# Weighing with high and low halves, four places for u, and scalings at the end of a batch, in a fused cross-attention and expert kernel

## The chip, the cores and the metric

One core of a Trainium2 chip. The metric is device microseconds from launch to end; lower is better. Engines: PE multiplies (with a weight-load side, PEld), DVE is the vector engine, ACT the activation engine, POOL the GpSimd engine, and SP issues every DMA of this kernel.

## The reference

`x` is 32 batches of 128 tokens of width 128, `ctx` 32 batches of 128 context rows of width 64.

```python
x = x + tanh(g_xattn) * (softmax(heads(ln(x) @ Wq) @ heads(ctx @ Wk).T / 8) @ heads(ctx @ Wv) @ Wo + bo)   # 16 heads of 64
x = x + tanh(g_ffn) * (shared_mlp(ln(x)) + routed_mlp(ln(x)))   # 32 experts of width 64; 8 picked out of 2 of 4 groups
```

## The kernel before, in words

**The products are folded.** Wq and Wk are folded per head at the start, and so are Wv and Wo (`c_pair`). So for each batch the scores are `ctx` times a projection `g` of the normalised tokens; the weights `p = exp(scores - max)` are applied to the raw context rows (`ctx_keys`, with a column of ones that gives the sum of the weights); the result `u` is divided by its sum and multiplied with `c_pair`.

**Formats.** Most products are made of three fp32r products, high*high + low*high + high*low, of operands that were split beforehand (`split_product`, L1148). Two products take plain f32 operands: `weigh` (L1219, u = keys x p) and `project_out` (L1245). A plain f32 product appears in the trace as two matmul records.

**Stages.** After a set-up of some 20 us come eight chunks of CB = 4 batches (`attention`, written once for each engine). The first and the last chunk are written out; chunks 1 to 6 (24 batches) are the body of a hardware loop (`in_chunks`, L238), the steady chunks. Then eight chunks of 17 expert units follow (`experts_of`), from about 355 us on. Batches b = 1 and 3 of a chunk are called odd here, b = 0 and 2 even.

**The order of the work is written out by hand**; each engine runs its list in order, with semaphore waits. In batch t:

- PE (L1287): `max_scores` of t+2 for the first half of the heads (h = 0), `scores` of t for h = 0, `transpose_max` of t+1, `weigh` of t-1 for h = 1 (two products, q = 0 and 1), in b = 1 `transpose_norm`, `project_out` of t-3, `max_scores` and `scores` for h = 1, `weigh` of t for h = 0, q = 0; in odd batches `g_project` of the next chunk into banks 0 to 3; `weigh` of h = 0, q = 1. `g_project` waits for `take_max` and `exp`, which empty its banks. The products of the next batch that write into banks 0 to 3 wait until `g_low` has read them (`glo_ready`, L1181 and L1203).
- ACT (L605): two `exp_of` of h = 0, `max_out`, two `u_out` of t-1 for h = 1 (copies of u from its bank into `u_raw`), in b = 1 `xt_high`, two `exp_of` of h = 1, `u_out` of t for h = 0, q = 0, in odd batches four `g_high`, `u_out` of h = 0, q = 1. `u_raw` has two places, so `u_out` waits until `normalise` has read what was there two batches ago (L548).
- DVE (L997): two `take_max` (L788) for h = 0, `normalise` of t-2 for q = 0 (L802, u times the inverse sums), in b = 1 `xt_low`, two `take_max` for h = 1, `invert` of t-1 (L796), `normalise` of t-2 for q = 1, in odd batches four `g_low` (L780), `residual` of t-3, statistics; in b = 0 `ln_apply` of the next chunk.
- POOL (L497): splits the expert weights (L468) and the context (L457), adds a bias.
- SP (L350): `load_max_row` of t+1, `spread_sums` of t-1 (L297), loads of context, expert weights and keys, `store_inverse` and `spread_inverse` of t-1 (L310): the sums go through a small DMA to `sums`, DVE inverts them, they are stored to DRAM and read back spread over partitions into `inverse_bc`, which has one place. All these pass through one queue in order.

`wbc` (L169) holds routing weights in the expert stage and is idle in the attention stage; so are the second parts of `x2t_hi`, `x2t_lo`, and the last columns of `w_hi`, `w_lo` until the last chunk.

Of the kernel before, what the change touches and what calls it, by code (L numbers as in the profile page):

```python
# [28 lines left out]
ALU = mybir.AluOpType  # L29
AX_X = mybir.AxisListType.X  # L30

P = 128
# [37 lines left out]
STATS_AT = {2: (2,), 3: (3,), 4: (4,), 5: (5,), 6: (6, 7)}  # L70
NB_SEAM = (NCH - 2) * CB
SEAM = {4: (1, 6), 5: (6, 10), 6: (10, 14), 7: (14, 21)}
LATE = {NB - 2: 3, NB - 1: 12}
NORM_AT = {(9, 1): ((NB - 1, 0),), (10, 1): ((NB - 1, 1),)}


def build(nc, x, ctx_nat, ctx_t, g_xattn, g_ffn, wq_t, wk_t, wv_t, wo, bo, router_t, router_bias, experts, out):
    with ExitStack() as stack:
# [42 lines left out]
        u_raw = (u_even, u_odd)  # L121
# [33 lines left out]

        spare = sb("spare", [P, 2 * CB * NE])
# [12 lines left out]
        wbc = sb("wbc", [P, WBC_SLOTS, 2, CT])  # L169
        rows_dram = nc.dram_tensor("rows_dram", (NCH, NE, CT), F32, kind="Internal").ap()  # L170
# [32 lines left out]
        st_done, exp_ready = sem("st_done"), sem("exp_ready")  # L203
        u_done, u_ready, inverse_ready = sem("u_done"), sem("u_ready"), sem("inverse_ready")
        norm_ready = [sem("norm_even_ready"), sem("norm_odd_ready")]
        sums_in, inverse_out, inverse_in = sem("sums_in"), sem("inverse_out"), sem("inverse_in")
# [66 lines left out]
        def _(sp):  # L273
# [23 lines left out]
            def spread_sums(t, parity):  # L297

                wait_first(u_ready, 4 * t + 4)
                for q in range(2):  # L300
                    row = CD if q == 0 else 0
                    sp.dma_start(sums[rows(q), parity, :], u_raw[parity][row:row + 1, q, :, :]).then_inc(sums_in, 16)
# [7 lines left out]
            def spread_inverse(t, parity):  # L310

                wait_first(inverse_out, 16 * t + 16)
                for q in range(2):
                    wait_first(norm_ready[q], t)
                for q in range(2):
                    sp.dma_start(inverse_bc[rows(q), :, :].rearrange("p h n -> p (h n)"),
                                 inverse_dram[parity, q:q + 1, :].broadcast_to([HD, 2 * CT])).then_inc(inverse_in, 16)
# [32 lines left out]
            def attention(c, first, last):  # L350
                for b in range(CB):
# [3 lines left out]
                    if not (first and b == 0):  # L355
                        spread_sums(t - 1, (b - 1) % 2)
# [64 lines left out]
            spread_sums(NB - 1, (NB - 1) % 2)  # L421
# [21 lines left out]
        def _(pool):  # L443
# [23 lines left out]

            def split_weights(slot, t, nth, contexts):  # L468
# [28 lines left out]
            def attention(c, first, last):  # L497
                for b in range(CB):
                    t = CB * c + b
                    split_weights(b % 2, t, 2 * c + b // 2, NB if last else t + CB)  # L500
# [24 lines left out]
        def _(act):  # L525
# [19 lines left out]
            def u_out(t, parity, h, q):  # L545
# [4 lines left out]
                nc.scalar.activation(u_raw[parity][held, q, h, :], u_ps[q][held, :], ACT.Copy).then_inc(u_ready, 1)  # L550
# [53 lines left out]

            def attention(c, first, last):  # L605
                for b in range(CB):
# [11 lines left out]
                    if not last and b == 1:  # L618
                        xt_high(c + 1)
# [7 lines left out]
                    u_out(t, b % 2, 0, 0)  # L627
                    if b % 2 == 1 and not last:
                        g_high(2 * c + 2 + b // 2, b // 2)
                    u_out(t, b % 2, 0, 1)  # L630
# [11 lines left out]
            u_out(NB - 1, (NB - 1) % 2, 1, 0)  # L642
            nc.scalar.activation(gates[:], tanh_g[:], ACT.Silu)
            u_out(NB - 1, (NB - 1) % 2, 1, 1)
# [44 lines left out]
        def _(dve):  # L689
# [105 lines left out]

            def invert(t, parity):  # L796
# [5 lines left out]
            def normalise(t, parity, q):  # L802

                dve.wait_ge(inverse_in, 32 * t + 32)
                wait(dve, attn_done, t - 1)
                nc.vector.tensor_tensor(u_t[rows(q), parity, :, :].rearrange("p i n -> p (i n)"),  # L806
                                        u_raw[parity][rows(q), q, :, :].rearrange("p h n -> p (h n)"),
# [189 lines left out]
            def attention(c, first, last):  # L997
                for b in range(CB):
                    t = CB * c + b
                    for h in range(2):  # L1000
# [7 lines left out]
                        if h == 1:  # L1008
                            if first and b >= 2:
                                normalise(t - 2, b % 2, 0)  # L1010
                            if not (first and b == 0):
                                invert(t - 1, (b - 1) % 2)
                            if not (first and b < 2):
                                normalise(t - 2, b % 2, 1)
# [5 lines left out]
                        if h == 1 and b % 2 == 1 and not last:  # L1020
# [11 lines left out]
                        elif not last and step_of_chunk == 1:  # L1032
                            ln_apply(c + 1, t - b + CB)
# [9 lines left out]
                        if h == 0 and not first:  # L1043
                            normalise(t - 2, b % 2, 0)
                        if step_of_chunk == 2 and not last:
                            xt_low(c + 1)
# [6 lines left out]
            in_chunks(dve, attention)  # L1053
            residual(NB - 3)
            normalise(NB - 2, (NB - 2) % 2, 0)
            invert(NB - 1, (NB - 1) % 2)
            normalise(NB - 2, (NB - 2) % 2, 1)


            def levels_at(c, parity, u, place, first, last):  # L1060

                if first:
                    for t, q in NORM_AT.get((u, place), ()):
                        normalise(t, t % 2, q)
# [82 lines left out]
        def _(pe):  # L1147
# [70 lines left out]

            def weigh(t, b, h, q, loads):  # L1219
# [67 lines left out]
            def attention(c, first, last):  # L1287
                for b in range(CB):
# [33 lines left out]
                    weigh(t, b, 0, 0, c + 1)  # L1322
# [4 lines left out]
                    weigh(t, b, 0, 1, c + 1)  # L1327
# [120 lines left out]
```

## Time and profile before

| | us |
|---|---|
| median of 3 runs | 664.85 (664.69 to 665.27) |
| the profiled execution, its own time | 668.55 |
| span of the profiled execution, first to last instruction | 666.8 |

| engine | busy us | share of the span |
|---|---|---|
| PE | 650.9 | 98% |
| DVE | 498.9 | 75% |
| ACT | 365.3 | 55% |
| POOL | 284.6 | 43% |

Read the profile from the stage inwards: busy shares by stretch, then the engines' lists in order of time over one pair of batches, with "idle before" in brackets and what ended it. The duration of a matmul record holds its latency, and records of neighbours overlap; what a matmul costs PE is the distance from its start to the next start.

### The profile page before, as it was taken

Reading aid. Unit: us, or ns where it says so; the run is one execution under the profiler, and the core shown is the slowest. Engines: PE = TensorE matmul, PEld = TensorE weight load, DVE = VectorE, ACT = ScalarE, POOL = GpSimd, SP = SyncE. Lnnn points to the kernel's source line nnn. Section 1 sums busy time; section 2 is a strip of 40 time slices with the busy share of each in tenths; the row PEclk is TensorE's granted clock in tenths of the full one; section 3 lists DMA queues with packets and bytes.
Section 4 is the critical chain, followed back from the end, with each engine's and each line's share of the span. In section 5 each row is a group of like instructions: output and inputs, shape, how many; then the busy total and the mean of one; then the engine's idle time right before and its main releaser. Section 6 shows DMA issues by size and latency. Waiting matters only on the chain.

```text
span 666.8 us, 13629 instructions
## 1 busy us (share of the span) xinstructions
PE 650.9 (98%) x3668; PEld 473.2 (71%) x3668; DVE 498.9 (75%) x1331; ACT 365.3 (55%) x690; POOL 284.6 (43%) x316
## 2 busy tenths in 40 slices
PE   8999999999999999999999999999999999999997
PEld 6656656667666666666657778788887878888785
DVE  6989858677586776776787968969596877869565
ACT  3564555465455555555465455555655655555553
POOL 4222323133132322234212655656565666657553
PEclk9999999999999999999999999999999999999999
DMA  8323322232323323233224825273654527374550
GB/s 188 94 64 82 92 63 70 63 91 63 80 62 79 94 62 79 62 79 83 63 67 130 192 62 134 83 170 99 141 133 98 134 72 164 81 162 112 131 142 16
DMA packets 63276, 65.58 MB, mean 98 GB/s; under 512 B 26112, under 2 KB 41600, under 8 KB 63232
## 3 DMA queue, kind: packets, MB, share of 16 engines
q1 hardware_dynamic: 63232, 65.07, 40.0%
q8 instruction: 18, 0.29, 0.2%
q14 instruction: 26, 0.21, 0.1%
HBM read 61.64 MB, written 2.88 MB: 97 GB/s over the span
## 4 chain that ended last, share of the span: by engine, by line
PE 68%; issue 8%; DMA 6%; DVE 6%; SPq 5%; POOL 4%; ACT 2%; DVEq 0%; POOLq 0%; ACTq 0%
PE bank L1151 13%; PE bank L1152 13%; PE bank L1153 13%; PE bank L1227 9%; PE bank L1251 5%; POOL halves L516 4%; PE bank L1187 3%; DMA inverse_bc<-inverse_dram 3%; PE bank L1207 2%; SPq L294 2%; DMA sums<-area 2%; DVE halves L783 2%; PE bank L1216 2%; PE bank L1213 2%; PE bank L1210 2%
## 5 line engine op out<-in xcount | busy, mean ns | idle before, releaser
L516 POOL TENSOR_TENSOR halves<-area,halves 128x512 fp32r<-128x512 f32 x134 | 173.9, 1298 | 141.3 <-ACT halves L650 137.8
L663 ACT ACTIVATE area<-bank 128x512 f32<-128x512 f32 x136 | 81.4, 599 | 116.1 <-PE bank L1153 115.1
L602 ACT ACTIVATE area<-bank 128x512 f32<-128x512 f32 x128 | 69.5, 595 | 118.7 <-PE bank L1216 118.7
L1107 DVE TENSOR_TENSOR bank<-area,bank 128x512 f32<-128x512 f32 x128 | 88.6, 692 | 53.4 <-PE bank L1153 53.2
L1227 PE MATMUL bank<-area,ctx_keys 128*65 128x512 f32 (+1 forms) x256 | 124.7, 600 | 0.5 <-ACT u_odd L550 0.4
L1151 PE MATMUL bank<-x2t_hi,w_hi 128*128 128x512 f32 x272 | 110.2, 405 | 0.1
L1152 PE MATMUL bank<-x2t_hi,w_lo 128*128 128x512 f32 x272 | 107.2, 394 | 0.0
L1153 PE MATMUL bank<-x2t_lo,w_hi 128*128 128x512 f32 x272 | 106.3, 391 | 0.0
L462 POOL TENSOR_TENSOR ctx_hi<-ctx_raw,ones_col 128x128 fp32r<-128x128 f32 x32 | 19.7, 615 | 200.4 <-DMA ctx_raw<-ctx_t 200.4
L792 DVE TENSOR_REDUCE row_max<-bank 128x4 f32<-128x512 f32 x128 | 81.7, 680 | 27.2 <-PE bank L1187 22.9
L650 ACT ACTIVATE halves<-area 128x512 fp32r<-128x512 f32 x136 | 85.0, 625 | 14.1 <-DVE area L1118 13.6
L1118 DVE TENSOR_TENSOR area<-bank,wbc 128x512 f32<-128x512 f32 x128 | 86.3, 679 | 0.0
L806 DVE TENSOR_TENSOR area<-u_odd,inverse_bc 64x1024 f32<-64x1024 f32 x32 | 40.6, 1269 | 45.1 <-DMA inverse_bc<-inverse_dram 44.6
L1251 PEld LDWEIGHTS bank<-c_pair,area 128*128 128x128 f32 x512 | 61.3, 192 | 12.6 <-issue 10.1
L1227 PEld LDWEIGHTS bank<-area,ctx_keys 128*65 128x65 f32 (+1 forms) x256 | 37.2, 164 | 39.6 <-issue 38.7
L1251 PE MATMUL bank<-c_pair,area 128*128 128x128 f32 x512 | 62.6, 276 | 1.2 <-DVE area L806 1.2
L1151 PEld LDWEIGHTS bank<-x2t_hi,w_hi 128*128 128x128 f32 x272 | 51.2, 188 | 12.1 <-DVE area L1118 1.8
L1153 PEld LDWEIGHTS bank<-x2t_lo,w_hi 128*128 128x128 f32 x272 | 51.2, 188 | 11.9
L1152 PEld LDWEIGHTS bank<-x2t_hi,w_lo 128*128 128x128 f32 x272 | 51.2, 188 | 10.3
L1187 PEld LDWEIGHTS bank<-ctx_hi,halves 64*128 64x128 f32 x512 | 33.5, 187 | 30.2 <-issue 22.3
L1151 PE MATMUL bank<-halves,w_hi 128*128 128x512 f32 x136 | 54.4, 400 | 0.5 <-POOL halves L516 0.5
L1153 PE MATMUL bank<-halves,w_hi 128*128 128x512 f32 x136 | 53.9, 396 | 0.0
(129 smaller groups left out, 1088.1 us busy)
## 6 DMA issues: line engine op xcount, KB each, us to landing
wbc<-rows_dram SPq DMA_DIRECT2D x126, 256.0 KB, 4.4
inverse_bc<-inverse_dram SPq DMA_DIRECT2D x64, 256.0 KB, 3.9
w_raw<-experts SPq DMA_DIRECT2D x32, 102.0 KB, 2.0
ctx_raw<-ctx_t SPq DMA_DIRECT2D x32, 64.0 KB, 1.8
ctx_keys<-ctx_nat SPq DMA_DIRECT2D x32, 64.0 KB, 2.1
out<-area SPq DMA_DIRECT2D x7, 256.0 KB, 3.9
max_rows<-max_t SPq DMA_DIRECT2D x64, 4.0 KB
area<-wq_t SPq DMA_DIRECT2D x1, 512.0 KB, 4.6
```

Source lines behind the costliest of these rows:

```text
L516: nc.gpsimd.tensor_tensor(hid_lo[:, u % SLOTS, :], hid[:, u % HIDS, :], raw(hid_hi[:, u % SLOTS, :]), ALU.subtract).then_inc(hidlo_ready, 1)
L602: nc.scalar.activation(probs_t[:, k, :, :], st_ps[q][:].rearrange("p (h n) -> p h n", h=4), ACT.Exp)\
L650: nc.scalar.activation(hid_hi[:, u % SLOTS, :], hid[:, u % HIDS, :], ACT.Copy).then_inc(hidhi_ready, 1)
L663: nc.scalar.activation(silu_g[:, u % 2, :], gate_ps[u % 2][:], ACT.Silu).then_inc(silu_ready, 1)
L792: nc.vector.tensor_reduce(row_max[:, parity, first:first + 4], ps[q][:].rearrange("p (h m) -> p h m", h=4), AX_X, ALU.max)\
L1107: nc.vector.tensor_tensor(up_ps[u % UPS][:], silu_g[:, u % 2, :], up_ps[u % UPS][:], ALU.mult)\
L1118: nc.vector.tensor_tensor(hid[:, u % HIDS, :], up_ps[u % UPS][:], wbc[:, group % WBC_SLOTS, i, :], ALU.mult).then_inc(hid_ready, 1)
L1151: nc.tensor.matmul(ps, wh, xh, start=start, stop=False)
L1152: nc.tensor.matmul(ps, wl, xh, start=False, stop=False)
L1153: return nc.tensor.matmul(ps, wh, xl, start=False, stop=stop)
L1227: nc.tensor.matmul(u_ps[q][0:CD + 1 if q == 0 else P, :], keys, probs_t[:, k, :, :].rearrange("p i n -> p (i n)"), start=True, stop=True). ...
L1251: ins = nc.tensor.matmul(ps, u_t[:, parity, p, :], c_pair[:, p, :], start=p == 0, stop=p == PAIRS - 1)
```

## The change

Three things change in the steady chunks. The products `weigh` of h = 0 are made of three fp32r products of halves: ACT makes the high half of p (`probs_high`), DVE the low half (`probs_low`), POOL the halves of the keys (`split_keys`). `u_raw` gets four places, two of them in `wbc`. `inverse_bc` gets a semaphore for each q, and DVE runs a list of its own, `steady_attention`, with both `normalise` at the end of the batch. The `weigh` products of h = 1, and all of the first and last chunk, stay plain f32. At the expert stage's start the two last `normalise` move one unit earlier, and the first load into `wbc` waits for the `normalise` that reads there.

```diff
-NORM_AT = {(9, 1): ((NB - 1, 0),), (10, 1): ((NB - 1, 1),)}
+NORM_AT = {(8, 1): ((NB - 1, 0),), (9, 1): ((NB - 1, 1),)}
+        p_hi = [x[:, 1, :] for x in (x2t_hi, x2t_lo)]
+        p_lo = [x[:, 0, :] for x in (x2t_hi, x2t_lo)]
+        tail = slice(WCOLS - 2 * 3 * CD, WCOLS)
+        keys_hi, keys_lo = (w[:, tail].rearrange("p (s n) -> p s n", s=2) for w in (w_hi, w_lo))
-        u_raw = (u_even, u_odd)
+        u_raw = (wbc[:, 0:2, :, :], wbc[:, 2:4, :, :], u_even, u_odd)
...
             def spread_inverse(t, parity):
                 wait_first(inverse_out, 16 * t + 16)
                 for q in range(2):
                     wait_first(norm_ready[q], t)
-                for q in range(2):
                     sp.dma_start(inverse_bc[rows(q), ...], inverse_dram[...]).then_inc(inverse_in[q], 16)
...
             def load_unit_1():
+                for q in range(2):
+                    wait_first(norm_ready[q], NB - 2)
...
+            def split_keys(b, t, c):
+                pool.wait_ge(keys_in[b], 16 * c + 16)
+                wait(pool, u_done, 4 * (t - 2) + 4)
+                nc.gpsimd.tensor_tensor(keys_hi[:, b % 2, :], ctx_keys[:, b, :], ones_col[:].broadcast_to([P, 3 * CD]),
+                                        ALU.mult).then_inc(keyshi_ready, 1)
+                pool.wait_ge(keyshi_ready, t + 1 - HALVED_FROM)
+                nc.gpsimd.tensor_tensor(keys_lo[:, b % 2, :], ctx_keys[:, b, :], raw(keys_hi[:, b % 2, :]), ALU.subtract)\
+                    .then_inc(keyslo_ready, 1)
...
             def u_out(t, slot, h, q):
                 act.wait_ge(u_done, 4 * t + 2 * h + q + 1)
-                wait(act, norm_ready[q], t - 1)
+                if h == 0 and (not isinstance(t, int) or t >= CB):
+                    act.wait_ge(norm_ready[q], t - CB + 1)
...
+            def probs_high(t):
+                act.wait_ge(exp_ready, 4 * t + 2)
+                wait(act, u_done, 4 * t - 2)
+                for q in range(2):
+                    nc.scalar.activation(p_hi[q], probs_t[:, q, :, :].rearrange("p h n -> p (h n)"), ACT.Copy)\
+                        .then_inc(phi_ready, 1)
...
+                    if not first and not last and b % 2 == 1:
+                        probs_high(t)
+                        if b == 1:
+                            xt_high(c + 1)
                     if not (first and b == 0):
                         for q in range(2):
-                            u_out(t - 1, (b - 1) % 2, 1, q)
+                            u_out(t - 1, (b - 1) % CB, 1, q)
+                    if not first and not last and b % 2 == 0:
+                        probs_high(t)
...
+            def probs_low(t):
+                for q in range(2):
+                    dve.wait_ge(phi_ready, 2 * (t - HALVED_FROM) + q + 1)
+                    wait(dve, u_done, 4 * (t - 1) + q + 1)
+                    nc.vector.tensor_tensor(p_lo[q], probs_t[:, q, :, :].rearrange("p h n -> p (h n)"),
+                                            raw(p_hi[q]), ALU.subtract).then_inc(plo_ready, 1)
...
+            def steady_attention(c):
+                for b in range(CB):
+                    t = CB * c + b
+                    for q in range(2):
+                        take_max(t + 2, b % 2, 0, q)
+                    batch_stats(t - CB, b)
+                    if b == 0:
+                        ln_apply(c + 1, t + CB)
+                    probs_low(t)
+                    if b == 1:
+                        xt_low(c + 1)
+                    for q in range(2):
+                        take_max(t + 2, b % 2, 1, q)
+                    invert(t - 1, (b - 1) % 2)
+                    residual(t - 3)
+                    batch_mean(t - CB, b)
+                    if b == CB - 1:
+                        keep_means(t - b - CB)
+                    normalise(t - 2, (b - 2) % CB, 0)
+                    if b % 2 == 1:
+                        g_low(2 * c + 2 + b // 2, b // 2)
+                    normalise(t - 2, (b - 2) % CB, 1)
...
+            def weigh_halves(t, b, q):
+                if q == 0:
+                    pe.wait_ge(keyslo_ready, t + 1 - HALVED_FROM)
+                pe.wait_ge(phi_ready, 2 * (t - HALVED_FROM) + q + 1)
+                wait(pe, u_ready, 4 * (t - 1) + q + 3)
+                cols = slice(0, CD + 1) if q == 0 else slice(CD, 3 * CD)
+                ps = u_ps[q][0:CD + 1 if q == 0 else P, :]
+                nc.tensor.matmul(ps, keys_hi[:, b % 2, cols], p_hi[q], start=True, stop=False)
+                nc.tensor.matmul(ps, keys_lo[:, b % 2, cols], p_hi[q], start=False, stop=False)
+                pe.wait_ge(plo_ready, 2 * (t - HALVED_FROM) + q + 1)
+                nc.tensor.matmul(ps, keys_hi[:, b % 2, cols], p_lo[q], start=False, stop=True).then_inc(u_done, 1)
```

## Rows read from the trace of the kernel before

**Rows 1.** Busy time (count) in the steady stretch: PE, PEld, DVE, ACT, POOL; clock, DMA share, GB/s.

```profile
75.00:325.00 250.00, 245.43 (x1643) 162.17 (x1643) 179.17 (x332) 135.42 (x263) 73.04 (x120) 1.00 0.29 73
```

**Rows 2.** PE's timeline: start us, us, what; one steady chunk apart three times.

```profile
72.97 1.95 PE L1251 MATMUL bank<-c_pair,area 128*128 128x128 f32 x16
```

**Rows 3.** PE's timeline over one odd and one even batch, some rows left out.

```profile
200.84 0.60 PE L1158 MATMUL bank<-ident,xn 128*128 128x128 f32 x4
201.28 1.95 PE L1251 MATMUL bank<-c_pair,area 128*128 128x128 f32 x16
...
206.34 0.39 PE L1151 MATMUL bank<-xnt_hi,a_hi 128*128 128x256 f32 x1 [0.53 <-DVE row_max L792]
...
209.28 1.02 PE L1227 MATMUL bank<-area,ctx_keys 128*128 128x512 f32 x2
...
211.06 0.50 PE L1207 MATMUL bank<-halves,ctx_hi 64*128 64x512 f32 x2 [0.17 <-DVE halves L783]
...
212.29 1.88 PE L1227 MATMUL bank<-area,ctx_keys 128*65 128x512 f32 x4
214.01 1.95 PE L1251 MATMUL bank<-c_pair,area 128*128 128x128 f32 x16
215.89 0.66 PE L1187 MATMUL bank<-ctx_hi,halves 64*128 64x128 f32 x8
216.39 0.45 PE L1207 MATMUL bank<-halves,ctx_hi 64*128 64x512 f32 x2
...
217.46 1.93 PE L1227 MATMUL bank<-area,ctx_keys 128*65 128x512 f32 x4
...
221.00 1.45 PE L1227 MATMUL bank<-area,ctx_keys 128*65 128x512 f32 x3
```

**Rows 4.** PE's timeline in the expert stage: two fp32r products of 512 columns in a row.

```profile
640.54 0.39 PE L1152 MATMUL bank<-x2t_hi,w_lo 128*128 128x512 f32 x1
640.77 0.40 PE L1153 MATMUL bank<-x2t_lo,w_hi 128*128 128x512 f32 x1
```

**Rows 5.** DVE's timeline: end of a b = 3 batch, then the odd batch of rows 3.

```profile
188.95 0.28 DVE L816 TENSOR_TENSOR x_sb<-bank,x_sb 128x128 f32 x1
...
189.56 0.17 DVE L720 COPY mean_var<-mean_var_now 128x8 f32 x1 [0.24 <-DVE mean_var_now L715]
...
203.87 1.22 DVE L806 TENSOR_TENSOR area<-u_odd,inverse_bc 64x1024 f32<-64x1024 f32 x1 [3.01 <-DMA inverse_bc<-inverse_dram]
...
205.61 1.27 DVE L792 TENSOR_REDUCE row_max<-bank 128x4 f32<-128x512 f32 x2
...
207.08 1.41 DVE L806 TENSOR_TENSOR area<-u_odd,inverse_bc 64x1024 f32<-64x1024 f32 x1
...
208.52 2.48 DVE L783 TENSOR_TENSOR halves<-bank,halves 128x512 fp32r<-128x512 f32 x4
```

**Rows 6.** The same batches on POOL, ACT and SP's queue.

```profile
206.88 0.53 POOL L473 TENSOR_TENSOR w_hi<-w_raw,ones_col 128x204 f32 x1 [0.24 <-POOL ctx_lo L465]
...
207.44 2.64 ACT L536 ACTIVATE halves<-bank 128x512 fp32r<-128x512 f32 x4 [0.96 <-PE bank L1153]
...
212.36 1.09 ACT L602 ACTIVATE area<-bank 128x512 f32<-128x512 f32 x2 [1.43 <-PE bank L1216]
...
213.33 0.25 ACT L543 ACTIVATE max_t<-bank 16x128 fp32r<-16x128 f32 x1
...
214.21 0.60 ACT L550 ACTIVATE u_odd<-bank 128x512 f32<-128x512 f32 x1 [0.15 <-PE bank L1227]
...
215.36 1.17 SPq L302 DMA_DIRECT2D sums<-u_odd  x2
```

**Rows 7.** DMA issues: KB each, median us from issue to landing.

```profile
inverse_bc<-inverse_dram SPq DMA_DIRECT2D x64, 256.0 KB, 3.9
...
sums<-u_odd SPq DMA_DIRECT2D x32, 4.0 KB, 1.8
```

**Rows 8.** A costly group: busy us, mean ns of one; nearest to the new copies of p.

```profile
L650 ACT ACTIVATE halves<-area 128x512 fp32r<-128x512 f32 x136 | 85.0, 625 | 14.1 <-DVE area L1118 13.6
```

More of the change, by code:

```diff
@@ L70 @@
 STATS_AT = {2: (2,), 3: (3,), 4: (4,), 5: (5,), 6: (6, 7)}
+HALVED_FROM = CB
 NB_SEAM = (NCH - 2) * CB
@@ L301, in spread_sums @@
                     row = CD if q == 0 else 0
-                    sp.dma_start(sums[rows(q), parity, :], u_raw[parity][row:row + 1, q, :, :]).then_inc(sums_in, 16)
+                    sp.dma_start(sums[rows(q), slot % 2, :], u_raw[slot][row:row + 1, q, :, :]).then_inc(sums_in, 16)
             def store_inverse(t, parity):
@@ L499, in attention @@
                     t = CB * c + b
+                    if not first and not last:
+                        split_keys(b, t, c)
                     split_weights(b % 2, t, 2 * c + b // 2, NB if last else t + CB)
@@ L612, in attention @@
                         max_out(t + 1, (b + 1) % 2, 2 * c + (b - 1) // 2 + 1)
+                    if not first and not last and b % 2 == 1:
+                        probs_high(t)
+                        if b == 1:
+                            xt_high(c + 1)
                     if not (first and b == 0):
                         for q in range(2):
-                            u_out(t - 1, (b - 1) % 2, 1, q)
+                            u_out(t - 1, (b - 1) % CB, 1, q)
+                    if not first and not last and b % 2 == 0:
+                        probs_high(t)
                     if last and b == CB - 1:
                         x2t_out(1, scores_ps[1])
-                    if not last and b == 1:
-                        xt_high(c + 1)
+                    if first and b == 1:
+                        xt_high(1)
                     if last and b == 1:
@@ L1019, in attention @@
                                 chunk_stats(n)
-                        if h == 1 and b % 2 == 1 and not last:
+                        if h == 1 and b % 2 == 1 and first:
                             g_low(2 * c + 2 + b // 2, b // 2)
@@ L1043, in attention @@
                         if h == 0 and not first:
-                            normalise(t - 2, b % 2, 0)
-                        if step_of_chunk == 2 and not last:
-                            xt_low(c + 1)
+                            normalise(t - 2, (b - 2) % CB, 0)
+                        if step_of_chunk == 2 and first:
+                            xt_low(1)
                         if step_of_chunk == 3 and last:
@@ L1063, in levels_at @@
                     for t, q in NORM_AT.get((u, place), ()):
-                        normalise(t, t % 2, q)
+                        normalise(t, t % CB, q)
                 if first and place == 1:
@@ L1321, in attention @@
                     scores(t, b, 2 * c + b // 2, 1, 2 * c + b // 2 + 1, None)
-                    weigh(t, b, 0, 0, c + 1)
+                    if first or last:
+                        weigh(t, b, 0, 0, c + 1)
+                    else:
+                        weigh_halves(t, b, 0)
                     if last and b == 0:
@@ L1326, in attention @@
                         g_project(b // 2, c + 1, ((max_ready, 4 * (t + 2) + 3), (exp_ready, 4 * t + 3)))
-                    weigh(t, b, 0, 1, c + 1)
+                    if first or last:
+                        weigh(t, b, 0, 1, c + 1)
+                    else:
+                        weigh_halves(t, b, 1)
             pe.wait_ge(neg_ready, 2)
```

48 lines of the change are left out of this document (26 added, 22 removed).

## The prediction

> **What bounds the kernel now.** I read the profile from the stage inwards. The change touches the steady chunks alone, so the first view is busy time in that stretch [rows 1]: PE is busy in nearly all of it, at full granted clock; DVE, which gets new work, is busy 179 of 250 us (72%); ACT and POOL have more room. The second view is PE's own timeline, because only a shorter PE list or a removed stall of PE can move the end. The chunk period is (201.28 - 72.97) / 3 = 42.77 us [rows 2, 3]. A batch without projection and without a stall takes 221.00 - 212.29 = 8.71 us. An odd batch adds the projection, 209.28 - 206.34 = 2.94 us, and b = 1 adds its transposes, 201.28 - 200.84 = 0.44 us [rows 3]. So PE's work in a chunk is 4 x 8.71 + 2 x 2.94 + 0.44 = 41.16 us, and 1.61 us a chunk are stalls. Both kinds show in rows 3: the projection waits for the last maxima (0.53), and the first scores after it wait for `g_low` (0.17); a weight load held beside them makes the true gap of each longer than the bracket. The third view, DVE's timeline, says why the maxima are late: `normalise` had stood 3.01 us for `inverse_bc` from DRAM, and everything queued behind it, `take_max` too, was late [rows 5]. That is a wait on a DMA which the change moves away.
>
> **Part 1: weighing with halves, on PE.** A plain f32 product costs (214.01 - 212.29) / 2 = 0.86 us [rows 3]. Three fp32r products of 512 columns go at 640.77 - 640.54 = 0.23 each [rows 4], 0.70 with rounding. 0.16 saved x 2 products a batch x 24 steady batches = **-7.7 us**. The price of 0.23 is read elsewhere, with 128 weight columns, as most here have. Bounds: 0.86 if the plain rate stays (0 us), 0.69 as read (-8.2 us); I stand at -7.7. The other two weighings of a batch stay as they are.
>
> **Part 2: scalings at the end, four places.** `normalise` of t-2 now comes last in batch t. Its `inverse_bc` load (3.9 us to land [rows 7]) is issued about a batch earlier than it is read, even though each half now waits for the last scaling of the batch before. So the stall of the projection (its `take_max` is now behind no DMA of DRAM) goes. The copies of u wait for a scaling three batches back: nothing.
>
> **Part 3: what is late next.** In an odd batch the chain to the next scores is now sums, `invert`, `residual`, `normalise` of q = 0, four `g_low`. I walk it from zero at the first `scores` product, with the even batch of rows 3 as ruler (zero is 211.06). On ACT the two exponentials are through at 212.36 + 1.09, so 2.4, the maxima's copy at 2.5 [rows 6]. In odd batches `probs_high` comes next, ahead of the copies of u: two of 0.6 [rows 8] overlapped, to 3.65; in b = 1 `xt_high` to 4.2; then two copies of u (0.6 each [rows 6], overlapped), to 4.7 in b = 3 and 5.3 in b = 1. SP starts the `sums` issues 0.2 to 0.5 after (215.36 after 214.81), the second is 0.6 later, and lands in 1.8 to 1.9 [rows 6, 7]: **7.4** and **8.0**. The reciprocal, residual and mean take 0.6; in b = 3 `keep_means` adds 0.5 (from 188.95 to 189.56 is 0.6, where residual and mean alone are 0.3) [rows 5]. Then the scaling, 1.22 alone and 1.41 beside POOL; I take 1.35. Then `g_low`, 2.5 to the next scores (208.52 to 211.06) [rows 3, 5]. Sum: **12.4** in b = 3, **12.5** in b = 1. PE has no more work before those scores than 217.46 - 211.06 = 6.40, plus 0.70, 2.94 and 0.70, plus 0.50 for `max_scores` (215.89 to 216.39): 11.2, in b = 1 0.44 later, 11.7 [rows 3]. Stalls 1.2 and 0.8: **2.0 us a chunk where there were 1.6**, in all 6 x 0.4 = **+2.4 us**.
>
> Bounds of this term. From below it is ACT's emptying of the four banks: exponentials of h = 1 end at 6.6 + 1.1, a copy of u to 8.2, four `g_high` of 2.64 together to 10.8, the last `g_low` to about 11.6 [rows 6, 5]: 0.4 a batch, 0.8 a chunk, -4.8 us in all. From above, one POOL instruction of 0.53 us or more in front of DVE on top of the 1.41: rival C.
>
> **Part 4: edits that I cost at nothing, and their cover.** ACT gets 8 x 0.6 us a chunk beside some 55% of busy time. In even batches its copies of u come first, `probs_high` ends at 4.9, and ACT's next exponentials are due at 6.6. `probs_low` is two DVE instructions of some 0.6 each (the pace of the four `g_low`, 2.48 / 4 [rows 5]). In odd batches it runs from 3.1 to 4.4, before the maxima of h = 1 (5.5). In even batches it waits for ACT until 4.4 and ends at 5.7; `take_max` (207.08 - 205.61 = 1.5 with the reciprocal [rows 5]), residual, mean and two scalings follow to 9.9. The even batch is 8.4 long, so DVE enters the odd batch 1.5 late, and absorbs that before 3.1. PE needs the low halves of p at 6.9, the maxima at 4.8 of the next batch: covered by over 1 us. If `probs_low` came after 6.9, each us would be PE's, 24 times. `project_out` of the next batch (due at 3.0) needs the last scaling, done at 1.5 after an even and at 12.4 + 1.4 - 12.4 = 1.4 after an odd batch. POOL gets 48 splits of 192 columns (nearest row 0.53 for 204 [rows 6]), 0.5 to 1.4 us with waits; it is busy 30% of the stretch, and the keys' halves are due at 6.4 of a batch that POOL begins near its start. SP issues nothing more, but ends each batch on the wait for the last scaling, with `load_max_row` queued behind; the scaling ends near 1.4, that load is wanted from 2.5 (213.33 + 0.25), and its rows at the next scores. The earlier last scalings move two DVE instructions one unit up, after their load has landed; the first load into `wbc` waits for a scaling of the last attention chunk, done long before the routing rows exist. First and last chunk: unchanged order.
>
> **The sum.** -7.7 + 2.4 = -5.3 against the profiled execution's span of 666.8, so 661.5. That execution's own time is 668.55, 3.7 over the median of the runs; the difference is carried to the median: 664.85 - 5.3 = **659.6 us**.
>
> **Rivals.**
> A, the forecast: 657 to 663, chance 0.48.
> B, the odd chain is shorter than walked and ACT's floor rules: -7.7 - 4.8 = -12.5, **652.4**. For it: my walk adds every semaphore and has the scaling beside POOL. Against: in both odd batches the sums land after the maxima are through, and DVE can't start `invert` sooner. Chance 0.20.
> C, slower: DVE gets in POOL's way in the odd batch. Place: the scaling and `invert` chain ahead of `g_low`. The row at 207.08 took 0.19 more than the usual 1.22 where a POOL split that had begun 0.2 before ran on for 0.33 [rows 5, 6]; now POOL has two more splits a batch, and its burst starts when the context lands, near the scaling. If each odd chain pays 0.7 more (a POOL split of 0.5 and another partly), the stalls are 2.0 + 1.4 = 3.4 a chunk: -7.7 + 6 x 1.8 = +3.1, **667.9**. It decides from 5.3 / 12 = 0.44 us more an odd batch: no wide margin. Against: the nearest row pays 0.19, and DVE is at (179 / 250 x 42.77 + 8 x 0.6) / 41.6 = 85%, so it is not full. Chance 0.19.
> D, the halves don't do what they say: three fp32r products with their own weight loads cost as much as the plain one. Then only the +2.4 stays, **667.2**. Against: rows 4 have a new weight load at each product too. Chance 0.05. The rest, 0.08, is between A and C, about no change.
>
> On C, the Trainium skill ("SBUF — State Buffer", Who interferes with whom) says that a DVE instruction with two SBUF inputs and a GpSimd instruction that reads SBUF exclude each other, the second waiting for the whole of the first. `probs_low`, `normalise` and `split_keys` are all of that kind, so by that rule C is likelier than the one row says; were a whole split paid each time, the sum would be C's. The trace agrees in kind, but shows 0.19 for 0.33 of overlap.
>
> **How the numbers follow.** The time is A's. The range reaches from B to just short of C: 652.5 to 666.5. About 0.2% (1.3 us) is what a measurement of this kernel can tell from no change. Faster by more: B and nearly all of A, 0.69. Slower by more: C, D's part, 0.20. Within: 0.11.
>
> **What would show each step.** After, PE's timeline should have a plain batch of 8.4 us and no idle before the projection on `row_max`; idle before the first scores after it, on `g_low`, of 0.8 in b = 1 and 1.2 in b = 3; DVE no idle on `inverse_bc` to speak of, some on the copies of p in even batches and on `sums` in odd ones; a chunk period near 41.9. Wrong would be: idle of PE in front of the third product of `weigh_halves`; scalings of 1.6 us and more beside POOL; the maxima's rows late at `scores`; a period over 42.8.

## The result, and the profile after

The changed kernel takes 660.78 us (median of 6 runs, 659.83 to 663.07) against 664.77 for the kernel before (6 runs): 4.0 us less, ratio 0.9939 (95% interval 0.9926 to 0.9953). The forecast was 659.6, in a range of 652.5 to 666.5. Two executions far above their like, one of 691.12 us in e3 and one of 3623.77 us of the kernel before beside e0 to e3, are left out of the medians and ratios below.

The profiled execution of after has a span of 658.9 us and a time of 661.07. First the busy time in the steady stretch, as in [rows 1] (PE, PEld, DVE, ACT, POOL, then granted clock, DMA share, GB/s):

```profile
75.00:325.00 250.00, 243.64 (x1733) 175.36 (x1730) 219.76 (x383) 160.32 (x315) 130.39 (x167) 0.99 0.28 75
```

DVE went from 179 to 220 us of the 250, POOL from 73 to 130, and the clock shows 0.99 where it was 1.00. PE is busy slightly less in a stretch that now holds more batches. Next PE's timeline over one odd batch (b = 1) and one even batch, to set beside [rows 3]:

```profile
195.38 0.45 PE L1276 MATMUL bank<-halves,ctx_hi 64*128 64x512 f32 x2
...
201.09 0.45 PE L1276 MATMUL bank<-halves,ctx_hi 64*128 64x512 f32 x2
...
202.16 0.44 PE L1296 MATMUL bank<-x2t_hi,w_hi 128*65 128x512 f32 x1
202.44 0.40 PE L1297 MATMUL bank<-x2t_hi,w_lo 128*65 128x512 f32 x1
202.68 0.39 PE L1299 MATMUL bank<-x2t_hi,w_hi 128*65 128x512 f32 x1
202.91 0.28 PE L1220 MATMUL bank<-xnt_hi,a_hi 128*128 128x256 f32 x1
...
207.45 0.50 PE L1276 MATMUL bank<-halves,ctx_hi 64*128 64x512 f32 x2 [0.25 <-DVE halves L820]
...
212.78 0.45 PE L1276 MATMUL bank<-halves,ctx_hi 64*128 64x512 f32 x2
...
215.89 0.45 PE L1276 MATMUL bank<-halves,ctx_hi 64*128 64x512 f32 x2
```

L1276 is the first `scores` product, twice a batch. In the even batch the second half now takes 215.89 - 212.78 = 3.11 us, where the same stretch took 3.43 to 3.44 in both profiles of before: 0.32 saved. The projection (202.91) starts right behind the first weighing, with no idle on `row_max`. What is left is the gap before 207.45, on `g_low` (L820). DVE's list of the same odd batch, beside [rows 5]:

```profile
199.37 1.10 DVE L838 TENSOR_TENSOR x2t_lo<-area,x2t_lo 128x512 fp32r<-128x512 f32 x1
200.39 0.68 DVE L815 TENSOR_TENSOR xnt_lo<-bank,xnt_hi 128x512 fp32r<-128x512 f32 x1
201.29 1.29 DVE L829 TENSOR_REDUCE row_max<-bank 128x4 f32<-128x512 f32 x2 [0.23 <-PE bank L1256]
203.23 0.25 DVE L845 RECIPROCAL inverse<-sums 128x16 f32<-128x16 f32 x1 [0.65 <-DMA sums<-wbc]
203.45 0.29 DVE L861 TENSOR_TENSOR x_sb<-bank,x_sb 128x128 f32 x1
...
203.79 1.22 DVE L851 TENSOR_TENSOR area<-u_odd,inverse_bc 64x1024 f32<-64x1024 f32 x1
204.93 2.47 DVE L820 TENSOR_TENSOR halves<-bank,halves 128x512 fp32r<-128x512 f32 x4
```

The 3 us on `inverse_bc` are gone; DVE now waits 0.65 us for `sums`, and from there every instruction up to the last `g_low` is on the path to 207.45.

**The measure used from here on** is the chunk period: the mean distance of the first `scores` product of h = 1 in b = 1 from one chunk to the next, over four chunks from about 118 us on. It leaves out two of the six such distances between chunk 1 and chunk 7, the first and the last; where they matter, all six are added up. For after it is (283.04 - 119.06) / 4 = 41.00 us, for the first profile of before (289.06 - 119.08) / 4 = 42.50.

### The profile page after: what moved, and what is told of

It is laid out like the page before. It is cut to its first block, busy times and chain, and to the rows that moved or that the text cites. A ratio compares the mean times of both kernels' runs of the same rounds, so it can differ in the third digit from the quotient of the medians.

```text
span 658.9 us, 13957 instructions
## 1 busy us (share of the span) xinstructions
PE 642.4 (97%) x3716; PEld 482.5 (73%) x3716; DVE 540.0 (82%) x1379; ACT 389.6 (59%) x738; POOL 344.7 (52%) x364
## 4 chain that ended last, share of the span: by engine, by line
PE 68%; issue 9%; DVE 6%; ACT 5%; DMA 4%; POOL 4%; SPq 2%; DVEq 1%; ACTq 0%; POOLq 0%
PE bank L1220 13%; PE bank L1221 13%; PE bank L1222 13%; PE bank L1309 7%; PE bank L1333 5%; POOL halves L538 4%; DVE halves L820 3%; PE bank L1256 3%; PE bank L1276 3%; DMA sums<-wbc 2%; PE bank L1285 2%; PE bank L1279 2%; PE bank L1282 2%; DMA sums<-area 1%; SPq L311 1%
## 5 line engine op out<-in xcount | busy, mean ns | idle before, releaser
L472 POOL TENSOR_TENSOR ctx_hi<-ctx_raw,ones_col 128x128 fp32r<-128x128 f32 x32 | 27.4, 858 | 137.7 <-DMA ctx_raw<-ctx_t 137.7
L1309 PE MATMUL bank<-area,ctx_keys 128*65 128x512 f32 (+1 forms) x160 | 77.8, 607 | 0.0
L1221 PE MATMUL bank<-halves,w_lo 128*128 128x512 f32 x136 | 53.5, 393 | 0.0
L1256 PE MATMUL bank<-ctx_hi,halves 64*128 64x128 f32 x512 | 42.1, 284 | 4.7 <-DVE halves L820 2.3
```

What stands on the lines that cost most here:

```text
L1221: nc.tensor.matmul(ps, wl, xh, start=False, stop=False)
L1256: ins = nc.tensor.matmul(ps[q][:, i * P:(i + 1) * P], g_hi[rows(q), (b // 2) % 2, 4 * h + i, cols], ctx_hi[rows(q), b % CB, :], start=True ...
L1309: nc.tensor.matmul(u_ps[q][0:CD + 1 if q == 0 else P, :], keys, probs_t[:, k, :, :].rearrange("p i n -> p (i n)"), start=True, stop=True). ...
```

## The experiments

Ratios are to the kernel before on the same chip, with 95% intervals; the medians come from different chips: after (the kernel before there: 664.77), e0 to e3 (665.8), e4 to e7 (666.15), e8 to e11 (665.73). Compare ratios across them, not medians. All rows but e0 have the four places and the semaphores for each q, and all but e0 and e2 the last scalings moved earlier; "old" and "new" mean DVE's list alone.

| kernel | order of DVE's list | halves | median us | ratio | period us |
|---|---|---|---|---|---|
| before, second profile (e0) | old | no | 666.42 (one run) | | 41.97 |
| e6 | old | yes | 667.40 | 1.0020 (1.0006 to 1.0033) | 42.13 |
| e1 | new | no | 662.36 | 0.9946 (0.9925 to 0.9967) | 41.39 |
| after | new | yes | 660.78 | 0.9939 (0.9926 to 0.9953) | 41.00 |
| e4, after again | new | yes | 662.17 | 0.9937 (0.9924 to 0.9951) | 41.04 |
| e5 | new, residual late | no | 662.50 | 0.9943 (0.9929 to 0.9956) | 41.38 |
| e3 | new, residual late | yes | 656.65 | 0.9861 (0.9837 to 0.9886) | 40.42 |
| e7 | as e3, `g_high` first on ACT | yes | 657.95 | 0.9876 (0.9861 to 0.9891) | 40.41 |
| e11 | new, copies of u first on ACT | yes | 657.86 | 0.9884 (0.9864 to 0.9903) | 40.57 |
| e2 | new, last scalings back | yes | 661.87 | 0.9938 (0.9916 to 0.9959) | 41.06 |
| e8 | new, one more op, odd | yes | 676.77 | 1.0155 (1.0116 to 1.0193) | 44.23 |
| e9 | new, one more op, even | yes | 661.72 | 0.9941 (0.9926 to 0.9957) | 41.20 |
| e10 | new, keys split once | yes | 661.45 | 0.9944 (0.9924 to 0.9963) | 41.00 |

**e0, the kernel before again.** No edit.

> The kernel before, unchanged, for a second profiled execution. The first one (668.55 us) was 3.7 us over the median of its runs, and its steady chunks were 42.5 us apart where the changed kernel's are 41.0. Theory: the extra 3.7 us lay in the steady chunks (late DRAM transfers of the inverse sums), so that this execution shows a chunk period near 42.0 and a gap of about 1.0 us a chunk to the changed kernel. Rival: the period is 42.5 again, and the difference lies outside the steady chunks.

Two rows of PE's timeline of e0, four chunks apart:

```profile
118.40 0.45 PE L1207 MATMUL bank<-halves,ctx_hi 64*128 64x512 f32 x2
...
286.28 0.45 PE L1207 MATMUL bank<-halves,ctx_hi 64*128 64x512 f32 x2
```

The period is (286.28 - 118.40) / 4 = 41.97: the execution that the prediction was made from stood 0.5 us a chunk longer than this one. So the theory holds. The stalls are 41.97 - 41.16 = 0.81 us a chunk here and 42.50 - 41.16 = 1.34 in the execution that the forecast read. The 1.61 of the forecast has 0.27 more, because its three chunks from 72.97 us on took in the long first distance (43.73 in that profile).

**e1, without the halves** (the new order, the four places, the semaphores for each q and the earlier last scalings stay).

```diff
-                    probs_low(t)                 # and probs_high, split_keys
-                    if first or last:
-                        weigh(t, b, 0, 0, c + 1)
-                    else:
-                        weigh_halves(t, b, 0)
+                    weigh(t, b, 0, 0, c + 1)     # and q = 1 alike
```

> The changed kernel with the halves taken out (all four weighings plain f32, no copies of p, no split of the keys), but with the four places and both scalings at the end of the batch. Theory (the halves save 0.32 us of PE work a batch, 7.7 us in all, and cost part of it back as stalls after the projection): 3 to 4.5 us slower than the changed kernel, so 664 to 665.3, with PE idle before the first scores after a projection of about 0.3 us a batch where the changed kernel has 0.4 and 0.8, and a chunk period of 41.5 to 41.8. Rival (the gain is the order's, the halves give nothing): about 661.

Its ratio, 0.9946, is hardly to be told from after's 0.9939. The period (41.39) is 0.4 above after's and just under the theory's 41.5 to 41.8, but the time is 1.6 us below its range, and the ratio only 0.0007 (0.5 us) above after's. Both were partly right. Over all six distances e1 takes 249.7 us, after 250.6 and e4 250.1: the halves pay in the four middle ones, and the long first one of after (below) takes that back. On the other side e1's profile has a wait in the expert stage that only e5's profile shares:

```profile
PE bank L1211 <- DVE area L1178: 0.8, 1, 0.8
```

From the last `project_out` to the end e1 takes 286.4 us, after 285.1. Why taking out the halves brings this wait is open.

**e6, the halves with the old order of DVE's list** (the four places, the semaphores for each q and the earlier last scalings stay).

```diff
                     batch_stats(t - CB, b)
-                    if b == 0:
-                        ln_apply(c + 1, t + CB)
+                    normalise(t - 2, (b - 2) % CB, 0)
                     probs_low(t)
...
                     invert(t - 1, (b - 1) % 2)
+                    normalise(t - 2, (b - 2) % CB, 1)
+                    if b % 2 == 1:
+                        g_low(2 * c + 2 + b // 2, b // 2)
                     residual(t - 3)
...
+                    if b == 0:
+                        ln_apply(c + 1, t + CB)
```

> The changed kernel with the halves and the four places, but DVE's list as before (scaling of q = 0 behind the first maxima, of q = 1 before g_low, ln_apply last). Theory (the order is what makes room for the halves): in odd batches the first scaling waits for inverse_bc until about 5.9 us after the first scores, the low halves come at 8.4 and the maxima at 10, so the projection starts near 10.3 instead of 7.5: up to 2.8 us for each of 12 odd batches, 680 to 695 us. Rival (the DMA's landing is not what binds, DVE catches up): 661 to 665.

667.4, a little slower than before: the direction of the theory and far from its size. In its waits (us in total, times, longest; five chunks):

```profile
DVE area L851 <- DMA inverse_bc<-inverse_dram: 19.2, 10, 3.0
...
PEld bank L1220 <- DVE row_max L829: 9.6, 9, 1.4
...
PE bank L1220 <- DVE row_max L829: 5.3, 9, 1.0
```

The projection does wait for the maxima, but by about 1 us and not 2.8. In its timeline the first scaling of an odd batch starts 202.20 - 197.52 = 4.7 us after the first scores, where my expectation had carried over 5.9 from [rows 5]. The loads are issued no sooner (1.1 us after the first scores, as in the first profile of before), but with a semaphore for each q the scaling waits for its own half alone: it starts 3.6 us after the first issue, where before's starts 4.8 after (4.5 in e0).

**e3, residual and statistics behind `g_low` in odd batches.**

```diff
                     invert(t - 1, (b - 1) % 2)
-                    residual(t - 3)
-                    batch_mean(t - CB, b)
-                    if b == CB - 1:
-                        keep_means(t - b - CB)
+                    if b % 2 == 0:
+                        residual(t - 3)
+                        batch_mean(t - CB, b)
                     normalise(t - 2, (b - 2) % CB, 0)
                     if b % 2 == 1:
                         g_low(2 * c + 2 + b // 2, b // 2)
+                        residual(t - 3)
+                        batch_mean(t - CB, b)
+                        if b == CB - 1:
+                            keep_means(t - b - CB)
                     normalise(t - 2, (b - 2) % CB, 1)
```

> The changed kernel with residual, batch_mean and keep_means behind g_low in odd batches. Theory (the chain sums, invert, residual, scaling, g_low ends last before the scores after a projection): the chain is 0.3 us shorter in b = 1 and 0.8 us in b = 3, the stalls of 0.4 and 0.8 fall to the floor that ACT's four copies of the projection set, about 0.3 each: 0.6 us a chunk, 657.2 us. Rival (ACT's copies or the sums' landing set it already): no change, 660.8.

656.65, ratio 0.9861: 9 us under the kernel before on the same chip, and the lowest ratio of the study. DVE in a b = 3 batch of e3:

```profile
178.26 0.25 DVE L845 RECIPROCAL inverse<-sums 128x16 f32<-128x16 f32 x1 [0.37 <-DMA sums<-area]
178.44 1.22 DVE L851 TENSOR_TENSOR area<-wbc,inverse_bc 64x1024 f32<-64x1024 f32 x1
179.84 2.74 DVE L820 TENSOR_TENSOR halves<-bank,halves 128x512 fp32r<-128x512 f32 x4 [0.18 <-ACT halves L558]
182.49 0.28 DVE L861 TENSOR_TENSOR x_sb<-bank,x_sb 128x128 f32 x1
```

Now `g_low` waits for ACT's `g_high` (0.18): the chain has come down to the floor, as expected. The period fell by 0.58, the expected 0.6.

**e5, e3 without the halves** (the edits of e1 and e3 together).

> The kernel with residual behind g_low in odd batches (656.9 us, chunk period 40.4), and with the halves taken out: all weighings plain f32. Theory (the halves are worth their 0.32 us of PE work a batch once the chain after the projection is short): the period is 41.3 us, 0.9 a chunk more, 5 us in all: 662. Rival (the halves give nothing either way; with the late residual the gain is all the order's): 657.

662.5 and a period of 41.38: as the theory had it. With the residual late, the halves are worth 41.38 - 40.42 = 0.96 us a chunk, and without them the late residual is worth nothing (41.39 and 41.38). The medians of e3 and e5 also hold e5's expert stage, which has the same wait of 0.8 us as e1's.

**e7, `g_high` ahead of the first copy of u**, on top of e3.

```diff
-                    u_out(t, b, 0, 0)
+                    if first or last:
+                        u_out(t, b, 0, 0)
                     if b % 2 == 1 and not last:
                         g_high(2 * c + 2 + b // 2, b // 2)
+                    if not first and not last:
+                        u_out(t, b, 0, 0)
```

> The kernel with residual behind g_low, and on ACT the copy of u for h = 0, q = 0 moved behind the four g_high. In its profile the last g_low waits 0.18 us for ACT. Theory (the floor of the stall after the projection is now ACT's start on the four banks): 0.1 to 0.2 us less in each odd batch, 1.2 to 2.4 us in all: 655. Rival (g_high waits for PE's first bank anyway, or the copies of u come too late for the next weighing): no change or slower, 656.9 or more.

The period is the same (40.41): the rival. With the copy gone from in front of it, ACT stands instead:

```profile
180.52 2.65 ACT L558 ACTIVATE halves<-bank 128x512 fp32r<-128x512 f32 x4 [0.47 <-PE bank L1228]
```

It starts 180.52 - 179.53 = 0.99 us after the projection's first product, in e3 179.21 - 178.22 = 0.99: the first bank sets the start, and the copy had fitted in front of it.

**e11, the copies of u ahead of the copies of p** in odd batches.

```diff
-                    if not first and not last and b % 2 == 1:
-                        probs_high(t)
-                        if b == 1:
-                            xt_high(c + 1)
...
-                    if not first and not last and b % 2 == 0:
+                    if not first and not last:
                         probs_high(t)
...
-                    if first and b == 1:
-                        xt_high(1)
+                    if not last and b == 1:
+                        xt_high(c + 1)
```

> The changed kernel with ACT's two copies of u ahead of probs_high in odd batches too, as in even ones (DVE's list as in the changed kernel). Theory (the sums of the odd batch land late because of the two copies of p ahead of them, 7.9 and 7.2 us after the first scores): the sums come up to 1 us sooner, DVE then is bound by its own list and starts invert 0.4 to 0.7 us sooner: stalls of 0.3 and 0.4, chunk period 40.5, 3 us less than the changed kernel: 659. Rival (the copies of p come too late for DVE then, and maxima and invert with them): no change, 662.

657.86 and a period of 40.57, against 659 and 40.5: the theory. The chain can be cut at its start (sums) as well as in its middle (residual); both end near the same floor. The two edits together were not tried.

**e8 and e9, one more DVE instruction** ahead of the first scaling, in odd or in even batches.

```diff
+                    if b % 2 == 1:               # e9: b % 2 == 0
+                        dve.wait_ge(c_ready, 2)
+                        nc.vector.tensor_tensor(x2t[:], c_pair[:, 0:4, :].rearrange("p h n -> p (h n)"),
+                                                c_pair[:, 4:8, :].rearrange("p h n -> p (h n)"), ALU.add)
                     normalise(t - 2, (b - 2) % CB, 0)
```

> The changed kernel with one more DVE instruction (128x512, two SBUF inputs, into a tile that nobody reads; 0.60 us at DVE's pace) ahead of the first scaling of each odd batch. Theory (the chain sums, invert, residual, scaling, g_low sets the scores after a projection): it comes through whole, 12 x 0.6 = 7.2 us over the changed kernel (662.2 on this chip): 669.4; stalls of 1.0 and 1.4 a chunk in place of 0.4 and 0.8. Rival (DVE waits for something else there, ACT's copies for instance): under 2 us.

> The same instruction ahead of the first scaling of each even batch. Theory (DVE enters the odd batch 1.5 us late and has time there before the low halves and the maxima of h = 1): nothing, 662.2. Rival (DVE is full at 88% busy, every instruction counts): 5 to 7 us more, as in the odd batches.

e9 costs nothing in time, 0.2 us a chunk in the period. e8 costs about twice the expected 7.2 us (by the ratios 14). PE's timeline of e8 around one b = 3 stall, and busy time and clock in three stretches of 2 us there (columns as above; the clock is the column before the last two):

```profile
195.02 0.66 PE L1260 MATMUL bank<-ctx_hi,halves 64*128 64x128 f32 x8 [1.15 <-DVE halves L820]
...
196.00 0.50 PE L1280 MATMUL bank<-halves,ctx_hi 64*128 64x512 f32 x2 [0.32 <-DVE halves L820]
...
197.52 3.22 PE L1313 MATMUL bank<-area,ctx_keys 128*65 128x512 f32 x4
200.58 1.95 PE L1337 MATMUL bank<-c_pair,area 128*128 128x128 f32 x16
```

```profile
196.00:198.00 2.00, 2.00 (x10) 1.08 (x11) 1.97 (x3) 0.47 (x1) 0.19 (x1) 0.70 0.02 6
198.00:200.00 2.00, 2.00 (x3) 0.67 (x2) 1.90 (x6) 1.27 (x4) 0.00 (x0) 0.50 0.34 129
200.00:202.00 2.00, 2.00 (x15) 1.67 (x14) 0.00 (x0) 1.29 (x4) 0.00 (x0) 0.95 0.03 6
```

The chain's part came through, and a little more than the 0.6 of the instruction: PE's stretch from the scores of h = 1 in an odd batch to the next scores grew from 6.36 to 7.09 (b = 1) and from 6.75 to 7.64 (b = 3), 1.6 us a chunk. But after each b = 3 stall of these four chunks the clock fell to 0.50, the lower of its two levels, and the next half batch took 6.95 us in place of 5.33: 1.6 us more a chunk. 44.23 - 41.00 = 3.2, which is the sum of the two.

**e2, the last scalings put back.**

```diff
-NORM_AT = {(8, 1): ((NB - 1, 0),), (9, 1): ((NB - 1, 1),)}
+NORM_AT = {(9, 1): ((NB - 1, 0),), (10, 1): ((NB - 1, 1),)}
```

> The changed kernel with the two last scalings put back one expert unit later. The profile of before has PE standing 1.2 us before a project_out in the expert stage, on a scaling; the changed kernel has 0.1. Theory: this edit, which the prediction costed at nothing, gives 1.2 us: this kernel at 662.0. Rival: the wait is hidden by what follows, 660.8.

In the waits of PE in the first expert chunk of e2:

```profile
PE bank L1333 <- DVE area L851: 1.2, 1, 1.2
```

The same wait stands in both profiles of before (on its lines, L1251 and L806) and in no other of the new `NORM_AT`. From the `project_out` after the attention stage to the last transposes, e2 takes 309.6 us, before 309.7 and after 308.5. So the edit gives 1.2 us in the profile. The ratio (0.9938, after's 0.9939) doesn't show it, and its interval is too wide to deny it.

**e10, the keys split once, outside the loop** (that write is not shown here), with other values, so that the first half of the heads is weighed with keys that are not the kernel's.

```diff
-                nc.gpsimd.tensor_tensor(keys_hi[:, b % 2, :], ctx_keys[:, b, :], ...).then_inc(keyshi_ready, 1)
-                pool.wait_ge(keyshi_ready, t + 1 - HALVED_FROM)
-                nc.gpsimd.tensor_tensor(keys_lo[:, b % 2, :], ctx_keys[:, b, :], ...).then_inc(keyslo_ready, 1)
+                pool.sem_inc(keyslo_ready, 1)
```

> The changed kernel with POOL's two splits of the keys left out of the loop (the halves of the keys are written once before it with other values; so the weighing of h = 0 is of those values). Theory (POOL stands in DVE's way only at single scalings, by 0.1 to 0.2 us): 0 to 1.5 us less than the changed kernel, 661 to 662.2. Rival, C of the prediction (a split in front of the scalings and the low halves costs the odd chain 0.3 us and more): 658.5 or less.

The period is 41.00, after's own. POOL's 48 new instructions cost the path nothing.

**e4, after again.**

> The changed kernel, unchanged, on the chip of the other three. In its first profile one steady chunk was 2.6 us longer than its neighbours: inverse_dram landed 1.1 us late near 90 us, PE stood 1.2 us before the scores after the projection, and the granted clock then fell to half for some 3 us. Theory: this is an event that comes in some executions only, so that the time is 659.5 to 661 with a spread of 2 us and more, and an execution at clock 1.0 is one of the short ones. Rival: it belongs to the kernel and is in every profile of it.

Its profile shows clock 1.0, a time of 660.86, and no half batch of 6.95. So the fall of the clock belongs to some executions, as the theory said. The theory's other half, that the late landing does too, is not borne out: see the last section. The median, 662.17, is over the expected 659.5 to 661, on a chip where before stands at 666.15; the ratio is after's.

## Why the prediction was right, point by point

**The weighing** (-7.7): right. 0.32 us a batch [rows 3 against 3.11 above]. The low halves ahead of it were costed at 0.6 us each; in odd batches the second takes 1.10 beside POOL (199.37 above) against 0.68 alone, but DVE waits 0.23 us for PE right after, so this is off the path.

**The stall before the projection**: gone, as forecast.

**The new chain**: right in place and order, too long in size. After the first scores of b = 1 (195.38), the walk had the reciprocal at 8.0, `g_low` at 9.95 and the next scores at 12.5; the rows show 7.85, 9.55 and 12.07. The oversized terms are the scaling (1.35 taken; 204.93 - 203.79 = 1.14 from its start to the next) and the landing of the sums. Against PE's own 41.16 - 4 x 0.32 = 39.88 us, after has 41.00 - 39.88 = 1.1 us of stalls a chunk, where 2.0 was forecast; at the two gaps of PE itself it is 0.4 in b = 1 and 0.8 in b = 3, where 0.8 and 1.2 were forecast. The forecast's sign of a period near 41.9 was missed with it. e8 shows that this chain sets the path, e3 and e11 that it can be cut at two places.

**The stalls before**: too large as well, 1.61 where e0 has 0.8 (the first paragraph on e0 says why). Two errors of the same sign stood in a difference: forecast 2.0 - 1.6 = +0.4 a chunk, measured in the middle chunks 1.1 - 0.8 = +0.3. That the difference came out was luck. By the forecast's own stretch, from b = 1 of chunk 1 to b = 1 of chunk 4, after even has (201.09 - 75.19) / 3 = 41.97 us, the 41.9 of the forecast; but it is made of 41.0 and of one late event, which the forecast did not have.

**The seam edit costed at nothing**: wrong. The cover I named, that the load had landed by then, was beside the point; PE's `project_out` waited for the scaling. It is 1.2 us of gain (e2), in plain sight in the profile of before as one wait, which I had not set against the edit.

**What is missing from the sum.** By the periods, 6 x (41.00 - 41.97) = -5.8 and -1.2 make -7.0, and the runs show -4.0. The two distances that the period leaves out hold the difference. From b = 1 of chunk 1 to b = 1 of chunk 2 (75.19 to 119.06) after's profile takes 43.87, 2.9 over its period, where e0's is 42.46, 0.5 over: that takes back 2.4 us. The last distance, which ends in the plain products of the last chunk, is 42.74 in after and 42.85 in e0, 1.7 and 0.9 over: that takes back 0.9. All six together are 250.59 against 253.19, so -2.6, and with -1.2 it is -3.8. So against e0 the steady chunks gave half of the forecast's -5.3: with -7.7 for the weighing the stalls cost +5.1, not +2.4. The seam, put at nothing, made up part of that, so 659.6 against 660.78 is nearer than its parts. Single profiles are no finer scale than this: by their spans after and e0 are 5.7 us apart, 0.6 of it ahead of the steady chunks and 1.3 in the last chunk, where nothing was taken apart.

**Rival C** (POOL in DVE's way by its two new splits): e10 speaks against it. Single scalings do go from 1.22 to 1.38 us beside POOL, but over the 40 scalings between 110 and 310 us the mean is 1.28 us in e10 and 1.27 in after, and the period is after's. The rule of exclusion in the Trainium skill ("SBUF — State Buffer", Who interferes with whom) is not contradicted. The trace agrees with it most plainly on POOL's side: in after a POOL split of 0.6 us that starts 0.17 us behind a scaling of 1.22 takes 1.54 (207.60). POOL has time for that; what the rule could have charged to the odd chain did not show in the period. **Rival B** (ACT's floor): not where the change went, but e3 and e11 came close to it. The stalls are 0.5 us a chunk in e3 (40.42 - 39.88), under the 0.8 that I gave as the floor. **Rival D** (the halves cost as much as the plain product): wrong, by the 0.32 us a batch that PE's timeline shows saved.

**Even batches**: e9 bears out that DVE, entering late, absorbs what it gets there.

## What to carry to other kernels

Where two lists run in lockstep, a cheaper product is worth its difference only if the other engine's chain gets shorter by as much: here the halves with the old list stood at 0.2% over the kernel before, the new list without halves at 0.5% under it, both together at 0.6%, and with a few small instructions moved off the chain at 1.4%. (Each of these has the four places and the earlier last scalings too, and what the four places and the semaphores for each q give by themselves was not measured.) Cost each end of a forecast difference from more than one execution, because stalls are just what differs between executions. And before an edit at a seam is called free, look for the wait that it shortens, not only for the cover of what it adds.

## What the runs showed of the hardware that I had not expected

**A stall can be charged twice.** After five of the six b = 3 stalls of e8 (stretches of 7.63 to 8.20 us against some 5.95 without one) and after its first b = 1 stall (8.41), PE's clock was granted at 0.50 (1.2 GHz) for about 3 us. The later b = 1 stretches of e8 (7.1) and its last b = 3 one (7.32) were not followed by it. In after it happened once, near 102 us, and in e2 once, behind a stretch of 7.58:

```profile
102.28 0.66 PE L1256 MATMUL bank<-ctx_hi,halves 64*128 64x128 f32 x8 [1.21 <-DVE halves L820]
103.26 0.50 PE L1276 MATMUL bank<-halves,ctx_hi 64*128 64x512 f32 x2 [0.32 <-DVE halves L820]
...
104.55 3.47 PE L1309 MATMUL bank<-area,ctx_keys 128*65 128x512 f32 x4
```

The four records of two plain products took 3.47 us where they take 1.88. But the size alone doesn't decide it. e10 has once the two gaps of e8 (1.15 and 0.32), in a stretch of 7.65 us, and stayed at clock 1.00:

```profile
103.84 0.66 PE L1257 MATMUL bank<-ctx_hi,halves 64*128 64x128 f32 x8 [1.15 <-DVE halves L821]
104.82 0.50 PE L1277 MATMUL bank<-halves,ctx_hi 64*128 64x512 f32 x2 [0.32 <-DVE halves L821]
...
106.06 1.88 PE L1310 MATMUL bank<-area,ctx_keys 128*65 128x512 f32 x4
```

Nor was it seen behind 7.52 in e4, 7.53 in e11 and 7.56 (b = 1) in e2, nor behind the 8.27 us stretch of before that ends near 104.6, which was made of two shorter gaps with the projection between them. What decides between 7.5 and 7.7 is open. The six executions of e8 run from 671.2 us at mean clock 0.995 to 680.7 at 0.982. As an estimate from these and from the trace, 0.013 of the clock over 676 us is five such falls, at 1.6 us each some 8 of the 9.5 us of spread.

**Transfers land late near the same place.** SP's queue of after near 90 us:

```profile
89.90 0.40 SPq L316 DMA_DIRECT2D inverse_dram<-inverse  x1
92.87 0.47 SPq L324 DMA_DIRECT2D inverse_bc<-inverse_dram  x1
```

From the store to the load behind it are 3.0 us; elsewhere in the same stage of this profile it is 1.6 to 2.0. In 12 of the 14 profiles of this study it is 2.3 to 3.1 us at this one store, between 89 and 94 us, and not in e0 and e1 (1.9 and 1.8). Elsewhere the other profiles have up to 2.2, e5 and e8 up to 2.6. SP stands meanwhile with `load_max_row` and `spread_sums` queued behind, which feed the odd chain. A kernel whose odd chain has room loses little there (e3's first distance is 40.61, 0.2 over its period). After's is 2.9 over in its first profile, 1.65 of that by the fall of the clock. In e4 it is 2.2 over, but 1.2 of this was lost at b = 1, before that store, where DVE stood longer for another transfer:

```profile
78.64 0.25 DVE L845 RECIPROCAL inverse<-sums 128x16 f32<-128x16 f32 x1 [1.55 <-DMA sums<-wbc]
```

The same wait is 0.41 us in the first profile of after. So late transfers near the start of the loop cost the changed kernel 2 to 3 us, and not one store alone. What makes them late stays open; nothing was tried on it.
